# Eight-layer kernel on one core: the 64-row heads' projections as products of split parts, made for two batches at once and further ahead, and 16-bit reads in the last layer

## The reference, cut to what matters

```python
# second layer, "l0f": causal attention, 16 heads of 64
xn = _rmsnorm(x, gamma1)
q = (xn @ q_w + q_b).reshape(b, s, H, HD).transpose(0, 2, 1, 3)   # k and v alike
q = _rope(q, theta); k = _rope(k, theta)
attn = softmax(where(causal, einsum('bhqd,bhkd->bhqk', q, k) * scale, -inf))
ctx = einsum('bhqk,bhkd->bhqd', attn, v)
attn_out = ctx @ o_w + o_b + xn
# last layer, "l3m"
x = act_qdq(x)                                   # to 16-bit steps and back
up = act_qdq(x @ lpbq_dequant(w_up).T)
gate = act_qdq(x @ lpbq_dequant(w_gate).T)
sig = fixed_qdq_u16(jax.nn.sigmoid(gate))
gate = act_qdq(gate * sig)
o = act_qdq(gate * up)
return o @ lpbq_dequant(w_down).T
```

## Time and profile before

| what | us |
|---|---|
| median of 3 runs | 1326.21 |
| lowest and highest | 1324.41, 1330.06 |
| the profiled execution's own time | 1321.66 |
| its span from first to last instruction | 1319.8 |
| PE busy over the span | 1160.2 (88%) |
| DVE busy | 995.9 (75%) |
| ACT busy | 875.7 (66%) |
| POOL busy | 560.5 (42%) |

### The profile page before, as it was taken

How to read it: one execution, slowest core, us unless ns; L and a number is a source line. 1 busy time by engine, 2 the same in 40 slices (tenths; PEclk the granted TensorE clock), 3 DMA queues, 4 the chain that set the end, 5 groups by cost and what they waited for, 6 DMA issues and landing times.

```text
span 1319.8 us, 29320 instructions
## 1 busy us (share of the span) xinstructions
PE 1160.2 (88%) x10082; PEld 894.7 (68%) x10082; DVE 995.9 (75%) x2234; ACT 875.7 (66%) x2403; POOL 560.5 (42%) x670
## 2 busy tenths in 40 slices
PE   7889889999988999997888899988999989997815
PEld 4677777788766788885666677766788666666403
DVE  6676677667758899997777766767666787887787
ACT  4666466656654799995888777764566447775684
POOL 5710366766653222255222231132877417881100
PEclk8999999999998999997999999998999899998967
DMA  5230000000002556650000010003222028750001
GB/s 168 60 93 16 20 2 2 2 3 2 2 2 87 181 210 212 209 208 1 2 2 2 3 42 2 2 2 114 88 88 84 0 55 206 190 139 1 1 0 33
DMA packets 38865, 83.71 MB, mean 63 GB/s; under 512 B 6066, under 2 KB 19762, under 8 KB 38740
## 3 DMA queue, kind: packets, MB, share of 16 engines
q1 hardware_dynamic: 38740, 82.07, 20.2%
HBM read 80.40 MB, written 1.64 MB: 62 GB/s over the span
## 4 chain that ended last, share of the span: by engine, by line
PE 59%; ACT 17%; DVE 14%; issue 7%; POOL 2%; DMA 1%; ACTq 0%; SPq 0%; POOLq 0%; DVEq 0%
PE score_bank L1662 18%; ACT h_all L1096 13%; PE f_bank L1696 6%; PE score_bank L1521 6%; PE f_bank L1422 4%; PE turn_bank L1537 4%; PE turn_bank L1696 3%; PE out_bank L1696 3%; PE out_bank L1577 2%; PE out_bank L1546 2%; DVE top_score L2006 2%; PE f_bank L1447 1%; DVE work L2018 1%; PE f_bank L1454 1%; DVE part_max L2404 1%
## 5 line engine op out<-in xcount | busy, mean ns | idle before, releaser
L1096 ACT ACTIVATE h_all<-score_bank,top_score 128x128 f32<-128x128 f32 x896 | 276.6, 400 | 101.3 <-DVE top_score L2006 101.2
L1662 PE MATMUL score_bank<-parts 128*128 128x512 f32 x1040 | 296.4, 403 | 9.8 <-DVE h_parts L2212 6.6
L1662 PEld LDWEIGHTS score_bank<-parts 128*128 128x128 f32 x1040 | 191.9, 190 | 75.2 <-DVE h_parts L2212 19.0
L2006 DVE TENSOR_REDUCE top_score<-score_bank 128x4 f32<-128x512 f32 x224 | 143.1, 681 | 105.2 <-PE score_bank L1521 105.2
L2212 DVE TENSOR_TENSOR h_parts<-score_bank,h_parts 128x512 fp32r<-128x512 f32 x260 | 178.3, 686 | 2.7 <-ACT h_parts L1211 2.4
L1211 ACT ACTIVATE h_parts<-score_bank 128x512 fp32r<-128x512 f32 x260 | 155.5, 598 | 31.8 <-PE f_bank L1696 8.5
L778 POOL TENSOR_TENSOR small<-small,half_neg 128x4 f32<-128x4 f32 (+4 forms) x24 | 36.6, 1528 | 177.0 <-DVE small L1981 83.2
L1537 PE MATMUL turn_bank<-CF,h_all 128*128 128x128 f32 x512 | 81.7, 283 | 30.3 <-DVE work L2018 19.0
L1537 PEld LDWEIGHTS turn_bank<-CF,h_all 128*128 128x128 f32 x512 | 56.1, 142 | 57.1 <-POOL h_all L803 18.1
L1188 ACT ACTIVATE score_bank<-score_bank,wset 128x512 f32<-128x512 f32 x128 | 84.6, 662 | 11.8 <-PE score_bank L1662 7.0
L2184 DVE TENSOR_TENSOR score_bank<-work,score_bank 128x512 f32<-128x512 f32 x124 | 86.3, 696 | 8.2 <-ACT score_bank L1188 5.6
(11 more groups left out here) (417 smaller groups left out, 2623.6 us busy)
## 6 DMA issues: line engine op xcount, KB each, us to landing
work<-gates_l0m SPq DMA_DIRECT2D x62, 512.0 KB, 3.9
W0X<-gates_l2m SPq DMA_DIRECT2D x32, 256.0 KB, 3.9
CTX<-gates_l2m SPq DMA_DIRECT2D x32, 256.0 KB, 3.9
wset<-in_l0m SPq DMA_DIRECT2D x32, 128.5 KB, 3.6
W0X<-gates_l1m SPq DMA_DIRECT2D x8, 512.0 KB, 3.8
wset<-in_l1m SPq DMA_DIRECT2D x8, 384.0 KB, 4.6
CTX<-gates_l1m SPq DMA_DIRECT2D x6, 512.0 KB, 4.0
big<-in_w0f SPq DMA_DIRECT2D x4, 512.0 KB, 3.9
```

The costliest lines, as they stand in the source:

```text
L1096: last = act.activation(held[c][:, P * m:P * m + P], score_bank[c][:, P * m:P * m + P], ACT.Exp, bias=top_score[c][:, m:m + 1], **sums)
L1662: last = pe_.matmul(bk[:, :], wt, y[:, x], start=(part == 0), stop=(part == len(parts_of) - 1))
L2006: dve.tensor_reduce(top_score[c][:, :], split(score_bank[c][:, :], HEADS), AX_X, ALU.max, negate=True)\
```

## The change

The `l0f` projections are made from split parts. The weights of queries, keys and values are cut once, by POOL in the setup, into a high part (fp32r) and the rest; the turned batch too: ACT copies the high part and DVE subtracts it to get the rest. A product is then three fp32r products (high by high, high by rest, rest by high). Queries and keys are made for two batches at once: the moving operand is 256 columns, two batches side by side, and side s = 0 makes the queries of both, side s = 1 the keys of both. So a job still fills one bank, and each batch still has four such jobs, but the scores of a batch wait for all eight of its pair. The table of the order moves F0 to two batches further ahead and F1 to F4 to one further, with special entries for the first two batches. POOL writes the results of a pair into three places each of `work`, and the turned probabilities move from there into `YT`. SP's bias rows come before its batch 9 instead of after its loop. In the last layer the step number is read as the lower 16 bits of the rounded value (every second 16-bit word), so `gate_steps` and `other` go, and DVE and ACT take their remaining pieces in another order.

```diff
-AWAY = {"before": -2, "last": -1, "own": 0, "next": 1, "after": 2}
+AWAY = {"before": -2, "last": -1, "own": 0, "next": 1, "after": 2, "first": 2, "second": 3, "third": 3, "fourth": 4}
+ONLY = {"first": [0], "second": [1], "third": range(1, 16), "fourth": range(2, 16)}
...
+        PE=[("F", 0, "first"), ("S", 0, "own"), ("F", 0, "second"), ("V", 1, "last"), ("F", 1, "first"), ("F", 2, "first"),
+            ("F", 3, "after"), ("F", 4, "after"), ("OP", 0, "last"), ("T", 0, "own"), ("F", 5, "next"), ("T", 1, "own"),
+            ("F", 6, "next"), ("F", 0, "fourth"), ("V", 0, "own"), ("T", 2, "own"), ("F", 1, "third"), ("T", 3, "own"),
+            ("F", 2, "third")],
...
+             ("R", 1, "own"), ("Y", 0, "fourth"), ("F", 4, "after"), ("C", 0, "own"), ("R", 2, "own"), ("OP", 0, "last"),
+             ("C", 1, "own"), ("F", 0, "fourth"), ("R", 3, "own"), ("F", 1, "third"), ("CX", 0, "own"), ("F", 2, "third")],
...
-        held_turned = [work[:, BANK * s + 4096:BANK * s + 4096 + BANK] for s in range(4)]
+        held_turned = [YT[:, BANK * s:BANK * s + BANK] for s in range(4)]
+        six = work[:, :].rearrange("p (n x) -> p n x", n=6)
+        q64_at, k64_at = [0, 1, 4], [2, 3, 5]
...
+        w0f_part = {"q": [parts[:, 0:1024], parts[:, 4096:5120]], "k": [parts[:, 1024:2048], parts[:, 5120:6144]],
+                    "v": [v_parts[:, :], parts[:, 2048:3072]]}
+        last_row = {"qa": Y[:, 0:8, :], "ka": Y[:, 8:B, :], "v": CTX[:, 0:8, :]}
...
+        def steps_in(t, at):
+            h = HIDDEN_ORDER[at]
+            return t[:, 1024 * h:1024 * h + 1024].bitcast(I16).rearrange("p (n two) -> p n two", two=2)[:, :, 0]
...
+                if b == 9:
+                    bias_rows()
...
+                        at = (q64_at, k64_at)[s]
+                        second = at[1 + i % 2]
+                        if i == 0:
+                            pool.wait_ge(scored, unit_no(LAYERS[0], PAIRS - 1, 1, 0) + LAYERS[0]["units"])
                         else:
-                            pool.wait_ge(scored, unit_no(L, i, s, 0) - L["units"])
-                        r, k = place(front_at[n], L["front"], i, s, u)
+                            pool.wait_ge(scored, unit_no(L, i - 1, 0, 0) + units)
+                        r, k = front_place(L, i, s, u)
                         pool.wait_ge(f_drained[r], k + 1)
-                        pool.tensor_tensor(dst[:, 0:BANK], rope_a[z][:, :], rope_c[z][:, :], ALU.subtract).then_inc(roped, 1)
-                        pool.tensor_tensor(dst[:, BANK:2 * BANK], rope_b[z][:, :], rope_d[z][:, :], ALU.add).then_inc(roped, 1)
+                        for half, (x, y, how) in enumerate(((rope_a, rope_c, ALU.subtract), (rope_b, rope_d, ALU.add))):
+                            cols = slice(BANK * half + 2 * P * m, BANK * half + 2 * P * m + 2 * P)
+                            dst = six[:, at[0]:second + 1:second - at[0], cols].rearrange("p e (c t) -> p c e t", t=P)
+                            pool.tensor_tensor(dst, x[m][:, :].rearrange("p (c e t) -> p c e t", c=2, e=2),
+                                               y[m][:, :].rearrange("p (c e t) -> p c e t", c=2, e=2), how).then_inc(roped, 1)
...
+            pool.wait_ge(in_bias, 16 * 5)
+            for n in ("q", "k", "v"):
+                high, rest = w0f_part[n]
+                link(pool.tensor_copy(high, w0f[n]))
+                pool.tensor_tensor(rest, w0f[n], high, ALU.subtract).then_inc(step("l0f.weights"), 1)
...
+                            act.activation(pair_part[i % 2][0][0:P - 1, P * t:P * t + P], bk[0:P - 1, 0:P], ACT.Copy)\
+                                .then_inc(pair_high_made, 1)
...
+                if at:
+                    sigmoid(at - 1)
+                    if at < 4:
+                        copies(0, at)
+            sigmoid(5)
+            act.wait_ge(step("l3m.scale"), 3)
+            for at in range(3):
                 rounded(U, at, 1, "l3m.u_round")
-            for at in range(2):
-                other(at)
             act.wait_ge(step("l3m.scale"), 4)
             for at in range(6):
                 rounded(big, at, 3, "l3m.round3")
-                if 1 <= at <= 4:
-                    other(at + 1)
+                if at < 3:
...
+                    rounded(U, at + 3, 1, "l3m.u_round")
...
+                        y_high, y_rest = pair_part[i % 2]
                         if u < 5:
-                            last = product(0, w0f["q" if u < 3 else "k"], 4 * ((u - 1) % 2), 4, yT1[t])
+                            if s == 0 and u == 1:
+                                if i == 0:
+                                    pe_.wait_ge(step("l0f.weights"), 6)
+                                    pe_.wait_ge(step("setup.ones"), 1)
+                                drained(i, 0, 0)
+                                drained(i, 1, 0)
+                            w_high, w_rest = w0f_part["qk"[s]]
+                            for c in range(2):
+                                at = 4 * ((u - 1) % 2) + 2 * ((u - 1) // 2) + c
+                                for w, y, first, end in ((w_high, y_high, True, False), (w_high, y_rest, False, False),
+                                                         (w_rest, y_high, False, True)):
+                                    last = pe_.matmul(bk[:, 2 * P * c:2 * P * c + 2 * P], w[:, P * at:P * at + P], y,
+                                                      start=first, stop=end)
                         else:
-                            last = pe_.matmul(bk[:, :], yT1[t][:, :], w0f["v"][:, BANK * (u - 5):BANK * (u - 5) + BANK], start=True, stop=True)
+                            w_high, w_rest = (w[:, BANK * (u - 5):BANK * (u - 5) + BANK] for w in w0f_part["v"])
+                            for w, y, first, end in ((w_high, y_high, True, False), (w_high, y_rest, False, False),
+                                                     (w_rest, y_high, False, True)):
+                                last = pe_.matmul(bk[:, :], y[:, P * t:P * t + P], w, start=first, stop=end)
...
-                        pe_.wait_ge(roped, 4 + 4 * s + 4 + 8 * i)
+                        pe_.wait_ge(roped, 4 + 8 * i + 8)
...
+                            which = s and 1 + i % 2
+                            queries, keys = six[:, q64_at[which], :], six[:, k64_at[which], :]
...
+                    if n == "l0f" and u == 0:
+                        high, rest = (part[0:P - 1, P * t:P * t + P] for part in pair_part[i % 2])
+                        dve.wait_ge(pair_high_made, b + 1)
+                        dve.tensor_tensor(rest, bk[0:P - 1, 0:P], high, ALU.subtract).then_inc(f_drained[r], 1)
...
-            def gate_steps(at):
-                dve.wait_ge(step("l3m.g_round"), at + 1)
-                dve.tensor_scalar(piece(big, at), piece(big, at), MAGIC, None, ALU.subtract).then_inc(step("l3m.g"), 1)
...
-                dve.scalar_tensor_tensor(piece(big, at), sg, MAGIC / 65536.0, piece(big, at), ALU.subtract, ALU.mult)\
+                dve.scalar_tensor_tensor(piece(big, at), sg, MAGIC / 65536.0, steps_in(big, at), ALU.subtract, ALU.mult)\
...
```

More of the change, by code:

```diff
@@ L15 @@
 U8 = mybir.dt.uint8
+I16 = mybir.dt.int16
 P = 128
@@ L182, in build @@
         POSF, HOT = CTX[:, 0:3, :], CTX[:, 3:6, :]
+        with nc.sbuf_tensor("pair_parts", [P, 9 * P], F32R) as pair_parts:
+            pass
         W3T = sb("W3T", [P, 9 * P])
+        pair_part = [[pair_parts[:, 512 * t + 256 * part:512 * t + 256 * part + 256] for part in range(2)] for t in range(2)]
         W3M = sb("W3M", [P, 36])
@@ L422, in place, with front_place @@
             return c % 2, per * i + c // 2 + 1
+        jobs0f = []
+        for own in range(-4, B):
+            for what, u, whose in ORDER["l0f"]["PE"]:
+                b = own + AWAY[whose]
+                if what == "F" and 0 <= b < B and b in ONLY.get(whose, range(B)):
+                    jobs0f.append((b, u))
+        def front_place(L, i, s, u):
+            if L["name"] == "l0f":
+                return place(front_at["l0f"], 0, 0, 0, jobs0f.index((2 * i + s, u)))
+            return place(front_at[L["name"]], L["front"], i, s, u)
         def front_use(name, c):
@@ L466, in work_of @@
                 return [(j / len(order), do, what, u, own + AWAY[whose]) for j, (what, u, whose) in enumerate(order)
-                        if 0 <= own + AWAY[whose] < B]
+                        if 0 <= own + AWAY[whose] < B and own + AWAY[whose] in ONLY.get(whose, range(B))]
             def steps(*layers):
@@ L621, in _, with bias_rows @@
             pieces[12] = lambda: load(WL2[:, :], a["wl2"], in_w1)
+            def bias_rows():
+                sp.wait_ge(step("l0f.weights"), 3)
+                sp.wait_ge(step("l0f.bias"), 2)
+                for n, at in (("q", 0), ("k", 16)):
+                    for half in range(2):
+                        sp.dma_start(w0f[n][P - 1:P, BANK * half:BANK * half + BANK].rearrange("o (n f) -> o n f", f=32),
```

(5 more changed lines are left out.)

113 lines of the change are left out of this document (41 added, 72 removed), and 1 row of the table DVE.

## The result

| | before | after |
|---|---|---|
| median of 5 runs, us | 1326.30 (1324.41 to 1330.06) | 1336.01 (1332.83 to 1344.17) |
| profiled execution: span, us | 1319.8 | 1334.1 |
| ratio after / before | | 1.0088, 95% interval 1.0050 to 1.0125 |
| the same on another chip, 11 runs | | 1.0075, 1.0045 to 1.0104 |

The change makes the kernel 0.8 to 0.9% slower, about 10 us. The prediction said 1331, with 1341 as its upper end: right sign and right range, half the loss missed. The two profiles show where the 14.3 us between the spans lie (the profiled execution of the kernel before was 4.6 us under its median, the one of after was the median, so 14.3 and not 10), and they answer to the groups shown ahead of the prediction.

The account below looks back on a forecast made before the run. PE's work (14.14 of 14.54 us a round) was taken as the bound, with chains only 0.40 and 0.8 us behind. +2.4 + 6.0 - 1.5 + 1.2 - 2.9 = +5.2 us on 1326.21 gave 1331, range 1318 to 1341.

Parts of the forecast that it names:

- Part 1: PE's projection jobs in l0f: 0.70 us each instead of 0.89 or 0.86, saving 1.1 us a batch.
- Part 2: Middle rounds of l0f: late reciprocal delays POOL's ropes, even scores 0.54 us later, odd 0.19 earlier; +2.4 us over seven pairs.
- Part 3: Fill and drain of l0f: jobs moved ahead of the first scores cost +6.0 us, bounds 0 and +8; drain counted separately.
- The drain: End of l0f: two rounds go without their query or key jobs; -1.5 us, bounds -3 and 0.
- the low bounds: All terms at their low ends, summed in the forecast to -9.2 us, giving 1317.
- Part 4: Setup beside l0x: POOL's weight splitting slows one or two of DVE's y_tok; +1.2 us, bounds 0 and +4.
- Part 5: Last layer: six gate_steps off DVE, less a longer wait for the first sigmoid; -2.9 us, bounds -3.6 and -1.5.
- A: Rival for the whole kernel: PE's work is the time, 16 batches save 1.1 us each, fill hidden; 1307, chance 0.06.
- B: Rival: POOL not late for even batches, -0.19 us each round, and the fill costs half; 1323, chance 0.20.
- C: Rival: POOL's ropes in l0f slower, 1.6 us instead of 1.23, from scattered 128-column writes; 1338, chance 0.20.

Follow-up runs that it names:

- e3: Kernel after with DVE's last reciprocal of a batch moved ahead of the subtraction for the rest of the turned batch; 1330.3 us, ratio to before 1.0042.
- e2: Kernel after with 32 extra PE products into an unused bank, in six places in the fill's waits; 1332.9 us, ratio to before 1.0060.
- e10: Kernel after measured again without an edit; 1336.4 us, ratio to before 1.0075.
- e4: e1 with ACT's first sigmoid directly behind the first rounding instead of behind the second; 1323.2 us, ratio to before 0.9979.
- e5: e3 with three more moves: DVE's y_tok before the second reciprocal, PE's last query job before the fourth turn, POOL's bias rows between scalings; 1327.3 us, ratio 1.0027.
- e7: Kernel before with one wait of PE made longer, DVE copying one turn bank of l0x four times instead of once; 1326.8 us, ratio 1.0020.
- e8: e4 with y_tok at the front of DVE's list and two query jobs ahead of PE's third and fourth turn; 1318.0 us, ratio to before 0.9943.
- e1: Kernel before with only the change's last layer (16-bit reads); 1321.3 us, ratio to before 0.9975.
- e9: e6 with extra PE products in two more waits, 10 before batch 0's first turn and 7 before batch 13's output product; 1324.7 us, ratio to before 1.0000.
- e6: e5 with the extra PE products of e2 and the earlier first sigmoid of e4; 1323.0 us, ratio to before 0.9991.

## Why the prediction was half right

**Part 1, 1.1 us a batch off PE: two thirds of it.** Six products of 256 columns take 0.79 us (265.77 to 266.56), against 0.89 before: 0.10, not 0.19. The 0.70 was read from three products of 512 columns; by columns alone six of 256 would take the same, and they don't. Why is not shown. Over batches 4 to 12 PE's busy time went from 113.09 to 107.03 us, 0.76 a batch.

**Part 2, the middle: mechanism right, +2.4 too much.** The reciprocal was put 1.17 late: it now stands 11.16 us behind the start of the scores (267.77 to 278.93) and stood 10.01 behind it before (265.17 to 275.18): 1.15 late. Even scores wait 0.66 for the ropes; a pair costs 0.17 and not 0.35, as an odd round gains 0.29 and not 0.19, so seven pairs make 1.2. e3 took the wait away and the unevenness went.

**Part 3, the fill: the step that failed.** It said "I take +6.0, bounds 0 (all in holes) and +8". With the clock held, e2 has +8.0: the upper bound. DVE's busy time in the fill grew by as much (13.41 to 21.38 us, where 6.6 was counted), so next to nothing of it went into the holes. What the step left out is that waits are not only lost time. It let the waits grow (2.75, 1.81 us) and priced the work behind them by rows at 2.4 GHz, while the chip granted 1.2. That gave +13.1. The first four rounds have it again: +2.6 in after, +1.5 in e10, +0.6 in e2, whose clock there was 0.97.

The clock's part in the profile of after is thus about 5.1 + 2.0 = 7.1 us, in that of e10 4.4 + 0.9 = 5.3. By this estimate the median would be 1329 to 1331 without it, which is the forecast. In part that is luck: the fill's jobs cost 2 us more than the 6.0 and the middle 1.2 less than the 2.4. The times of e2 bear out 2 to 4 us of it; the rest stands on the traces alone.

**The drain, -1.5: measured -1.3.** It is the sum of two rows of the table, +0.7 from batch 12 to 15 and -2.0 behind. They look so unlike since the clock fell once in each kernel's drain, one round apart: ahead of batch 15 in after, behind it in the kernel before.

```profile
385.57 3.37 PE L1588 MATMUL out_bank<-big,oT 128*128 128x128 f32 x16 [1.89 <-ACT oT L1120]
```

```profile
388.04 3.45 PE L1650 MATMUL out_bank<-big,oT 128*128 128x128 f32 x16 [1.89 <-ACT oT L1172]
```

The first line is the kernel before (output product of batch 14), the second after (of batch 13). At full clock the product takes 2.05 us, as it did behind the same wait in e3, e4, e5, e7 and e8. So the clock costs nothing here between the two kernels. (A slip of the sum: the low bounds add up to -9.3, not -9.2.)

**Part 4, +1.2 for POOL's splitting: +0.4, and partly by luck.** One y_tok was hit, at 75.70:

```profile
75.70 2.37 DVE L2126 TENSOR_SCALAR y_tok<-X,small 128x128 f32<-128x128 f32 x1
```

So were three of DVE's scalings, which the sum gave nothing: 1.25 us at 74.53, 1.19 at 80.77 and 1.65 at 84.18, for 0.69 in the kernel before. Together that is 4 us of DVE. Both agree with the Trainium skill's lock ("SBUF — State Buffer", section SBUF: two separate sides), by which a VectorE operation with two SBUF inputs waits too. But over the older part of the setup the kernel before had two y_tok of 2.4 us and one of 1.2, and after one of 1.2 only. Where the locks fall varies from kernel to kernel (e10 has a second y_tok of 2.40, at 66.15). The last scores of `l0x` stand between 140.5 and 143.8 us in the five kernels with the old products and between 139.0 and 142.1 in the seven with the new ones, so no price is to be seen. A cast took 1.03 to 1.50 us and a subtraction 2.35 to 2.67, as bounded from the earlier trace rows.

**Part 5, -2.9: measured -2.8.** The six subtractions of the earlier trace rows are gone, DVE waits 3.25 us for the first sigmoid, and 16-bit reads at stride 2 cost what fp32 did (rows of after's sigmoid and its product):

```profile
1276.78 1.15 ACT L1416 ACTIVATE CTX<-big,quant 128x1024 f32<-128x1024 int16 x1
```

```profile
1274.35 0.69 DVE L2539 TENSOR_SCALAR CTX<-CTX 128x1024 f32<-128x1024 f32 x1 [3.25 <-ACT CTX L1416]
1275.07 1.23 DVE L2540 SCALAR_TENSOR_TENSOR big<-CTX,big 128x1024 f32<-128x1024 f32 x1
```

**Rivals.** A needed equal rounds of 13.5, B of 14.3: after has neither. C needed ropes over the 1.23 us from start to start of the earlier trace rows; they took 1.24 (280.18 to 281.42), and the rest of C's 1338 was not there. The time came near C's for another reason, which no rival had.

## What to carry to other kernels

A prologue that makes work further ahead has waits, and behind them TensorE's clock can fall to half (here behind 1.4 and 1.9 us in some traces, behind 2.8 and 3.6 in those shown, for 3 to 7 us): price the fill as waits plus work at the lower clock, or fill the waits with products into a free bank, which here made a stretch 5 us shorter by adding work, and the kernel 2 to 4. When two profiles are compared row by row, look where the clock fell in each: a fall that only moved looks like a loss in one row and a gain in the next. Look for one instruction in front of a chain (a reciprocal behind a subtraction, a y_tok behind a maximum) before building new products: moving such places gave 4 to 6 us, and the new products, even reordered and kept warm, none by the time.

## What was not expected of the hardware

The clock may fall or not behind the same waits. In the last layer's start the code of before and of e1 is the same, and the waits ahead are the same (ScalarE's 1.39 us and TensorE's 2.38); before was granted 1.00 and e1 0.50 over six streamed products:

```profile
1234.00:1237.00 3.00, 3.00 (x20) 1.73 (x18) 1.83 (x5) 0.00 (x0) 0.00 (x0) 1.00 0.00 0
```

```profile
1239.00:1242.00 3.00, 3.00 (x10) 1.37 (x10) 1.25 (x3) 0.00 (x0) 0.00 (x0) 0.50 0.00 0
```

From the last tile's statistics to the first scale it is 6.8 to 6.9 us in before, after, e2, e5, e7 and e9, 8.5 in e6, and 9.7 to 9.8 in e1, e3, e4, e8 and e10. Why it falls in one and not in the other is not shown. It is one source of the scatter of single profiles, and a reason to attribute by stretch and not by span.
